# Attention block with output projection, RMS norm and residual: places of scalings, additions and low-part subtractions in slots 1, 2 and 5, and narrower waits of the evacuations

## The reference

```python
qkv = jnp.einsum('bchw,oc->bohw', x, w_qkv)          # 3 * 512 outputs
q, k, v = jnp.split(qkv, 3, axis=1)                  # 8 heads of 64; q is scaled by 64 ** -0.5
sim = jnp.einsum('bhdi,bhdj->bhij', q, k)
attn = jax.nn.softmax(sim, axis=-1)
out = jnp.einsum('bhij,bhdj->bhid', attn, v)
y = jnp.einsum('bchw,oc->bohw', out, w_out) + b_out
y = y * jax.lax.rsqrt(mean over channels of y * y + 64 ** -0.5) * rms_scale
return y + x
```

## Time and profile before

| | |
|---|---|
| median of 3 runs | 4412.9 us (4409.09 to 4414.07) |
| the profiled execution's own time | 4412.16 us |
| its span, first to last instruction | 4410.4 us |
| TensorE (PE) busy | 4146.6 us, 94% |
| VectorE (DVE) busy | 2866.3 us, 65% |
| GpSimd (POOL) busy | 2837.1 us, 64% |
| ScalarE (ACT) busy | 2266.8 us, 51% |
| mean granted TensorE clock | 0.975 |

### The profile page before, as it was taken

How to read it: one execution, slowest core, us unless ns; L and a number is a source line. 1 busy time by engine, 2 the same in 40 slices (tenths; PEclk the granted TensorE clock), 3 DMA queues, 4 the chain that set the end, 5 groups by cost and what they waited for, 6 DMA issues and landing times.

```text
span 4410.4 us, 53031 instructions
## 1 busy us (share of the span) xinstructions
PE 4146.6 (94%) x18624; PEld 2434.4 (55%) x18624; DVE 2866.3 (65%) x2700; ACT 2266.8 (51%) x3969; POOL 2837.1 (64%) x2188
## 2 busy tenths in 40 slices
PE   7999999999999999999999999999999999999996
PEld 5555555555555555555555655555555555555553
DVE  4666666666666666666676766666666666666665
ACT  3555455455555555454554545545555455454553
POOL 4566666666666656666666666667666666666666
PEclk8999999999999999999999999999999999999998
DMA  3111111111111111111011010110111111111110
GB/s 135 39 48 39 48 39 61 45 48 39 58 48 39 48 39 58 48 39 67 29 53 53 32 65 29 58 49 34 62 44 43 48 39 58 48 39 48 39 39 29
DMA packets 71270, 212.19 MB, mean 48 GB/s; under 512 B 8152, under 2 KB 8280, under 8 KB 58208
## 3 DMA queue, kind: packets, MB, share of 16 engines
q1 hardware_dynamic: 71008, 208.80, 13.3%
HBM read 168.92 MB, written 39.85 MB: 47 GB/s over the span
## 4 chain that ended last, share of the span: by engine, by line
PE 57%; issue 20%; POOL 13%; ACT 7%; DVE 3%; DMA 0%; POOLq 0%; ACTq 0%; SPq 0%; DVEq 0%
PE aux L442 12%; PE pv L587 12%; PE score L572 8%; POOL prob_sum L975 8%; PE aux L475 7%; PE score L574 6%; PE aux L499 5%; PE aux L553 5%; ACT probs L656 2%; POOL prob_sum L971 2%; POOL resid L988 1%; DVE rms_b L869 1%; PE aux L507 1%; POOL x_lo L285 1%; ACT q_hm L665 1%
## 5 line engine op out<-in xcount | busy, mean ns | idle before, releaser
L975 POOL TENSOR_TENSOR prob_sum<-prob_sum,probs 128x512 f32<-128x512 f32 x1536 | 1984.5, 1315 | 672.1 <-ACT probs L656 669.8
L831 DVE TENSOR_REDUCE maxima<-aux 128x1 fp32r<-128x1024 f32 x1024 | 1206.1, 1219 | 998.6 <-PE aux L553 928.3
L656 ACT ACTIVATE probs<-score 128x512 f32<-128x512 f32 x2048 | 1112.0, 594 | 990.5 <-PE score L574 982.9
L587 PE MATMUL pv<-probs,v_sb 128*64 128x512 f32 x4096 | 1005.6, 612 | 0.0
L572 PE MATMUL score<-q_hl,k_hh 128*128 128x512 f32 x2048 | 895.5, 437 | 8.2 <-ACT probs L656 6.4
L574 PE MATMUL score<-q_hm,k_l 72*128 72x512 f32 x2048 | 823.7, 402 | 0.0
L971 POOL TENSOR_TENSOR prob_sum<-probs 128x512 f32<-128x512 f32 x256 | 339.5, 1347 | 657.0 <-ACT probs L656 657.0
L442 PE MATMUL aux<-x_hi,w_ring 128*128 128x512 f32 x2048 | 668.6, 408 | 19.7 <-POOL x_lo L285 11.2
L572 PEld LDWEIGHTS score<-q_hl,k_hh 128*128 128x128 f32 x2048 | 392.8, 192 | 281.4 <-issue 178.9
L587 PEld LDWEIGHTS pv<-probs,v_sb 128*64 128x64 f32 x4096 | 251.9, 138 | 495.7 <-issue 428.7
L442 PEld LDWEIGHTS aux<-x_hi,w_ring 128*128 128x128 f32 x2048 | 359.2, 189 | 175.5 <-issue 66.4
(11 more groups left out here) (74 smaller groups left out, 4447.2 us busy)
## 6 DMA issues: line engine op xcount, KB each, us to landing
w_ring<-w_split SPq DMA_DIRECT2D x93, 1024.0 KB, 4.8
x_stage<-x SPq DMA_DIRECT2D x128, 256.0 KB, 4.1
resid<-x SPq DMA_DIRECT2D x128, 256.0 KB, 5.7
out<-resid SPq DMA_DIRECT2D x128, 256.0 KB, 2.0
w_split<-w_ring SPq DMA_DIRECT2D x3, 1024.0 KB, 12.0
w_split<-y_sb SPq DMA_DIRECT2D x3, 1024.0 KB, 3.8
y_sb<-wqkv SPq DMA_DIRECT2D x4, 512.0 KB, 8.7
probs<-wqkv SPq DMA_DIRECT2D x2, 512.0 KB, 7.8
```

The lines of the kernel that those rows point to most:

```text
L587: pe.matmul(pv[half][e * D:(e + 1) * D, :], v_sb[:, pair // 2, j, (pair % 2) * P + e * D:(pair % 2) * P + (e + 1) * D], probs[:, j % 4, e, ...
L656: act.activation(probs[:, j % 4, e, :], score[e][:], ACT.Exp, scale=SOFT).then_inc(prob_ready, 1)
L831: dve.tensor_reduce(maxima[:, n:n + 1], bank(k, 2), AX_X, ALU.max).then_inc(aux_free[k], 1)
L975: pool.tensor_tensor(prob_sum[:, e, :], prob_sum[:, e, :], probs[:, j % 4, e, :], ALU.add).then_inc(prob_added, 1)
```

## The change

Seven constants move work between places and engines, and one wait is narrowed. In slot 1 the scalings stand at t = 2, 3, 4, 6 instead of 2, 5, 7, 8; the first reciprocal of the sums stands at t = 2 instead of 3; the additions of x stand at steps 1 to 4 instead of 2 to 5. In slot 2 the additions of x stand at steps 1, 2, 4, 4 instead of 2, 3, 4, 5, and `o_lo` is made by GpSimd before its additions of j = 4 instead of by VectorE at t = 7. In slot 5 the split of x chunk 3 by GpSimd comes after the additions of j = 1 instead of j = 2, and both reciprocals of the sums stand at t = 5 instead of 2 and 5. ScalarE, which waited for all four additions of x of its half before O0, now waits before each of its four copies for the addition of its own m.

```diff
-INVERT_SUMS_AT = ((2, 5), (3, 5), (2, 5), (2, 2), (2, 5), (2, 5), (2, 2), (2, 2))
+INVERT_SUMS_AT = ((2, 5), (2, 5), (2, 5), (2, 2), (2, 5), (5, 5), (2, 2), (2, 2))
 NORMALISE_AT = (6, 6, 6, 4, 6, 6, 4, 4)
 OUTPUT_HIGH_AT = (7, 7, 7, 6, 7, 7, 6, 6)
-LOW_BY_GPSIMD = (0, 1, 3, 4, 5, 7)
+LOW_BY_GPSIMD = (0, 1, 2, 3, 4, 5, 7)
@@
-SCALE_AT = (((1, 2), (1, 5), (1, 7), (1, 8)), ((2, 2), (2, 3), (2, 6), (2, 8)))
-RESIDUAL_AT = ((2, 3, 4, 5), (2, 3, 4, 5))
+SCALE_AT = (((1, 2), (1, 3), (1, 4), (1, 6)), ((2, 2), (2, 3), (2, 6), (2, 8)))
+RESIDUAL_AT = ((1, 2, 3, 4), (1, 2, 4, 4))
@@
-SPLIT_LOW_AT = ((5, 1), (5, 0), (5, 3), (5, 4), (6, 5), (6, 6), (6, 9), (6, 12))
+SPLIT_LOW_AT = ((5, 1), (5, 0), (5, 3), (5, 2), (6, 5), (6, 6), (6, 9), (6, 12))
@@
-                    if name == "O0" and not body.first:
-                        act.wait_ge(resid_added, 4 * (2 * (body.b - 1) + half + 1))
                     if name == "O0" and body.first and half == 0:
                         act.wait_ge(spilled_t, 48)
                     for i in range(2):
                         m = 2 * int(name[1]) + i
+                        if not body.first:
+                            act.wait_ge(resid_added, 4 * (2 * (body.b - 1) + half) + m + 1)
                         ins = act.activation(y_sb[:, half, m, :], bank(k + i),
                                              ACT.Identity, bias=bias_sb[:, m:m + 1])
                     ins.then_inc(aux_free[k], 1)
```

## The result

The changed kernel takes 4197.2 us (median of 4 runs, 4196.7 to 4200.33) against 4412.96 us before: a ratio of 0.9514, 95% interval 0.950 to 0.9528. The forecast was 4193 us. The profiled execution has a span of 4195.5 us where it had 4410.4; the mean granted clock is 0.993 instead of 0.975.

The account below looks back on a forecast made before the run. TensorE, busy 94% of the span, plus its gaps was taken to bound the kernel. Slots 1 and 2 win 172 us, slot 5 49, the last batch loses 2: 219 us from 4412.16, hence 4193 us, range 4170 to 4240.

Parts of the forecast that it names:

- The frame: Slots 1 and 2 without gaps, judged from the first batch: 64.4 us instead of 77.04, so 12.6 us a batch to win.
- Slot 1: R no longer waits 5.6 us for ScalarE's copy and low clock goes: slot 1 at 33.4 us, 8.4 shorter.
- Slot 2: With `o_lo` on GpSimd, O0 starts 1.7 us sooner and 0.7 us of gap remains; slot 2 at 32.1 us.
- the 3.05 us that the prediction drew: In slot 2, the scores of j = 7 start 3.05 us sooner; bounds 1.7 to 3.9 us.
- Slot 5: V0 starts sooner after the moved split: 2.55 us plus 0.7 of clock a batch, 49 us; slot 5 at 29.4 us.
- The last batch: Its slot 5 has no V0 or split to gain from, only the later reciprocal: 1.7 us lost once.
- one of the signs of being wrong: In slot 5, TensorE waiting for exponentials would show the prediction wrong; no size given.
- The clock: TensorE's low clock goes with the gaps: mean granted clock 0.995 or more, none low where no gap is.
- The held scalings: Rival, 13%: early scalings meet more GpSimd instructions and hold up VectorE; some 3 us a batch lost, 4238 us.
- every gap closes: Rival, 12%: all gaps of slots 1, 2 and 5 go, 16.1 us a batch, 241 us, hence 4171 us.
- GpSimd as the bound: Rival, 3%: GpSimd's additions, all held, fall 3.2 us short in slot 1, 6.4 us in both slots: 4289 us.
- the clock on the slower side: Rival, 2%: gapless work in slots 1 and 2 gets 0.50 for long stretches; 4454 us at 35 us a batch.

Follow-up runs that it names:

- experiment 11: Experiment 10 plus, in slot 1, addition m = 2 after the additions of j = 4, and the last batch's first slot 5 reciprocal at t = 2: 4177.5 us.
- experiment 1: Kernel before with only the narrow wait: each of ScalarE's copies waits for its own addition of x; 4318.8 us, ratio 0.9789.
- experiment 2: Changed kernel with the old wait: O0's copies wait for all four additions of their half; 4235.9 us, ratio 0.960.
- experiment 3: Kernel before with only the moved scalings, first reciprocal of slot 1 and additions of x in slots 1 and 2; 4302.9 us, ratio 0.9754.
- experiment 10: Changed kernel with scaling m = 3 of slot 2 at t = 9, behind M2's maxima, instead of t = 8; 4185.2 us, ratio 0.9485.
- experiment 6: Changed kernel with `o_lo` of slot 2 back on VectorE at t = 7; 4230.8 us, ratio 0.9582.
- experiment 5: Changed kernel with the first reciprocal of slot 5 back at t = 2; 4225.2 us, ratio 0.9578.
- experiment 8: Changed kernel with GpSimd's split of x chunk 3 back after the additions of j = 2; 4234.9 us, ratio 0.9601.
- experiment 7: Changed kernel with all four scalings of slot 1 at t = 1 to 4, in front of M1's maxima; 4229.6 us, ratio 0.9587.
- slot 5 alone: Kernel before with only slot 5's two edits: split of chunk 3 after j = 1, both reciprocals at t = 5; 4361.5 us, ratio 0.9884.

## Why the prediction was right, point by point

**The frame.** The first batch as the measure of a slot without gaps held: experiment 11 reaches 33.13 + 31.57 = 64.7 us in slots 1 and 2, against the floor of 64.4.

**Slot 1** was forecast at 33.4 us and takes 33.44. Less 104.73 us, the events drawn in the old frame are M1's maxima at 2156.42, `o_lo` at 2164.2 and R at 2168.7; the trace has 2156.38, 2164.24 and 2168.66. That the 0.42 us wait of O0 stays was right in kind (0.28 us). Experiments 1 to 3 weigh the two edits, which the prediction priced only together: the narrow wait by itself closes R's gap, and the moves bring the last 0.74 us.

**Slot 2** was forecast at 32.15 us and takes 32.4. O0 waits 0.77 us (forecast 0.7), for the reason given, and experiment 10 shows it by taking the reason away. Of the 0.25 us more, most is in the 3.05 us that the prediction drew: slot 2 of the first batch, which has no gap there, takes 31.57 us, and 31.57 + 0.77 is already 32.34. One part was put down to the wrong edit. The prediction gave all the 1.7 us by which O0 came sooner to the move of `o_lo`. Experiments 3 and 6 have the gap at 1.56 us with `o_lo` on VectorE and the additions moved, so the additions bring 2.45 - 1.56 = 0.9 us and `o_lo` 1.56 - 0.77 = 0.8.

**Slot 5** was forecast at 29.4 us and takes 29.52. Experiments 5 and 8 show that the split and the reciprocal both were needed.

**The last batch** was forecast to lose 1.7 us and lost 3.2. TensorE waits 2.39 us for exponentials there. That it would wait for exponentials in slot 5 was one of the signs of being wrong, and in this one batch it came. The queue was drawn rightly, though: in experiment 10 the same 2.39 us gap stands with the clock up, and the slot takes 28.76 us, 1.7 more than before. What the forecast left out is the low clock behind the gap, 1.5 us (TensorE, timeline and window, changed kernel, then experiment 10):

```profile
4089.08 0.80 PE L572 MATMUL score<-q_hl,k_hh 128*128 128x512 f32 x1 [2.39 <-ACT probs L656]
4089.00:4092.00 3.00, 2.92 (x7) 0.50 0.00 0
```

```profile
4076.19 0.51 PE L572 MATMUL score<-q_hl,k_hh 128*128 128x512 f32 x1 [2.39 <-ACT probs L656]
4076.00:4079.00 3.00, 2.81 (x12) 1.00 0.00 0
```

**The clock** went as forecast where it matters: no stretch at 0.50 from the second batch to the last one's slot 5. The mean was forecast at 0.995 or more and is 0.993 (0.991 to 0.993 in the four executions); the low clock that is left stands in the first batch and from the last one's slot 5 on. But here the forecast was lucky. It took for granted, without a row, that small gaps leave the clock up. In the changed kernel 0.77 us does; behind 1.35 to 1.6 us the clock falls in 9, 14 and 10 of 15 batches in experiments 5 to 7, and a single scaling placed wrongly (experiment 7) costs 32 us, of which the gap itself is only some 16.

**The rivals.** The held scalings are real: three that meet GpSimd take 4.06 us, and with one more in front of M1 the time is 4230 us, 32 us above the changed kernel; in the change as made they just fit. That this is near the rival's 4238 is chance: the rival had three slots late by the queues alone, and here it is one slot, with the low clock in 10 batches making half of it. That every gap closes was 4171 us; 4177.5 us was reached with three more edits. GpSimd as the bound and the clock on the slower side did not come up: the page has GpSimd at 68%.

**The sum.** Forecast 172 + 49 - 2 = 219 us, measured 168 + 47 - 3 + 3 = 215.

## What to carry to other kernels

Where one engine is busy 94%, list its gaps, find for each the instruction that ends it last, and draw that engine's queue forward event by event from the durations of the trace; the length of a stage in an iteration that lacks the extra work says how much there is to win. Edits that shorten the same gap don't add: test them from both ends, one alone and one taken back. Two edits that only move where gaps fall can change which batches get the low clock, so count these batches, and don't read them off one. An engine that is slower at an operation can still be the right place for it, if its time is covered and the faster one's queue is on the path.

## What the runs showed of the hardware

The low clock is not a function of the gap in front of it. The count of batches with a stretch at 0.50 at or behind the gap, of 15, in the profiled execution of each kernel:

| kernel, gap of TensorE | us | batches with low clock |
|---|---|---|
| before and slot 5 alone, R in slot 1 | 5.66 | 15 |
| before, V0 in slot 5 | 2.77 | 7 |
| narrow wait alone, V0 | 2.77 | 15 |
| moves alone, V0 | 2.77 | 14 |
| split late, V0 | 2.77 | 0 |
| before, O0 in slot 2 | 2.45 | 8 |
| narrow wait alone and slot 5 alone, O0 in slot 2 | 2.45 | 15 |
| moves alone, R in slot 1 | 2.0 | 2 |
| old wait in the changed kernel, R | 2.0 | 5 |
| moves alone, O0 in slot 2 | 1.56 | 1 |
| `o_lo` on VectorE, O0 in slot 2 | 1.56 | 14 |
| four scalings first, V1 in slot 1 | 1.49 | 10 |
| early reciprocal, V0 | 1.35 | 9 |
| changed, O0 in slot 2 | 0.77 | 0 |

Where one kernel has batches of both kinds, the low clock makes the slot 1.3 to 1.6 us longer, about as much as the shorter of these gaps themselves; in three batches of experiment 3, where it lasted longer, 2.6 us; in slot 2 before only 0.45, since a later wait went. The same gap in the same kernel has it in some batches and not in others, and 1.56 us before O0 draws it once in one kernel and 14 times in another, so neither the gap's length nor the order of work decides. That it is where in time the gaps fall fits this, and no experiment shifted a gap in time alone, so it stays open. For a forecast it means that a gap of 1.35 to 2.8 us in this kernel has two prices, with and without 1.5 us, and that both belong into the range: my three largest misses (28 us in experiment 1, 13 us in experiments 5 and 7) are this term.

A VectorE instruction with two inputs in SBUF that comes while a GpSimd instruction runs ends about 0.55 us behind it: 0.69 us when none runs (`o_lo` in experiment 6), 1.59 and 1.78 us for held ones. With this one behaviour the events of slot 1 could be drawn to within 0.1 us.
